# Interleaving LayerNorm and its transposes with the Q, K and V projections, tile by tile, in an eight-core transformer layer on Trainium2

## The reference

```python
xn = _layernorm(x, axis=-1)
s = attn(xn, qw, kw, vw, ow)   # 16 heads of 64, rope on Q and K, causal softmax
g = _silu(moe(xn, Wg, We, be)) # 8 experts of 1024 x 1024, top 2 by xn @ Wg.T
x = x + s * g
```

## Time and profile before

| what | value |
|---|---|
| time, median of 3 runs | 3062.99 us (3062.61 to 3220.71) |
| the profiled execution | 3064.13 us |
| its span, first to last instruction, slowest core | 3062.6 us |
| spans of the eight cores | 3039.6 to 3062.6 us |
| PE / DVE / ACT / POOL busy | 72% / 35% / 32% / 18% |
| mean granted clock of PE | 0.873 of full speed |

### The profile page before, as it was taken

The page is one execution under the profiler, slowest core; times in us unless marked ns, Lnnn a source line. Parts: engine busy times, 40 slices in busy tenths (PEclk is TensorE's granted clock), DMA queues, the critical chain, the costliest instruction groups (busy, mean ns, idle before and its releaser), DMA issues.

```text
span 3062.6 us, 30462 instructions; the slowest of 8 cores (3039.6 to 3062.6 us)
## 1 busy us (share of the span) xinstructions
PE 2195.3 (72%) x9976; PEld 819.0 (27%) x9976; DVE 1066.2 (35%) x1560; ACT 965.4 (32%) x1373; POOL 539.9 (18%) x575
## 2 busy tenths in 40 slices
PE   1233498888499689959969990677778807777787
PEld 0113133333144234424424440112121201121212
DVE  3661466666244234414423440322121203121212
ACT  3550122222100200020020000565758504757584
POOL 0010178888100000000000000211111102211111
PEclk9999999999699799979979995588888856788888
DMA  4159522222733255073335408022010080220100
GB/s 128 45 76 111 70 97 104 104 104 104 138 56 56 64 91 94 1 137 56 56 77 94 78 1 209 12 69 69 1 56 1 1 194 1 69 69 1 55 1 28
DMA packets 380489, 212.37 MB, mean 69 GB/s; under 512 B 342944, under 2 KB 342944, under 8 KB 379824
## 3 DMA queue, kind: packets, MB, share of 16 engines
q1 hardware_dynamic: 365552, 142.76, 22.6%
q0 software_dynamic: 14784, 67.66, 10.1%
HBM read 92.67 MB, written 67.37 MB: 52 GB/s over the span
## 4 chain that ended last, share of the span: by engine, by line
PE 44%; DVE 12%; ACT 11%; SPq 8%; issue 8%; POOLq 5%; DMA 5%; POOL 5%; DVEq 0%; ACTq 0%
PE PA L654 15%; PE PB L654 14%; ACT AR L838 8%; SPq L238 7%; PE PV L757 5%; POOLq L92 5%; POOL AR L849 5%; PE PA L883 4%; DMA AR<-c_sin 3%; PE PA L828 2%; PE PB L828 2%; DVE AR L550 2%; ACT AR L767 2%; DVE AR L556 2%; DVE AR L548 2%
## 5 line engine op out<-in xcount | busy, mean ns | idle before, releaser
L654 PE MATMUL PA<-AR 128*128 128x512 f16 x2048 | 469.9, 383 | 23.8 <-DMA AR<-we 23.8
L757 PE MATMUL PV<-AR 128*128 128x512 f16 (+6 forms) x1280 | 416.6, 416 | 66.4 <-POOL AR L849 66.3
L654 PE MATMUL PB<-AR 128*128 128x512 f16 x2048 | 462.9, 379 | 0.0
L838 ACT ACTIVATE AR<-PA 128x1024 f16<-128x1024 f32 x320 | 303.2, 948 | 250.6 <-PE PA L828 248.5
L828 PE MATMUL PA<-AR 64*128 64x512 f16 x640 | 148.7, 456 | 300.4 <-DMA AR<-q_sp 145.8
L664 DVE SCALAR_TENSOR_TENSOR AR<-PA,wm,AR 128x512 f32<-128x512 f32 x256 | 192.1, 750 | 423.1 <-PE PA L654 222.3
L849 POOL TENSOR_TENSOR AR<-AR,tri 128x256 f16<-128x256 f16 x256 | 171.2, 669 | 821.3 <-ACT AR L838 797.8
L838 ACT ACTIVATE AR<-PB 128x1024 f16<-128x1024 f32 (+1 forms) x320 | 276.3, 864 | 90.4 <-PE PB L828 90.3
L664 DVE SCALAR_TENSOR_TENSOR AR<-PB,wm,AR 128x512 f32<-128x512 f32 x256 | 192.1, 750 | 249.3 <-PE PB L654 230.9
L654 PEld LDWEIGHTS PA<-AR 128*128 128x128 f16 x2048 | 202.0, 99 | 271.5 <-issue 34.9
L799 DVE TENSOR_TENSOR AR<-AR,PC 64x512 f16<-64x512 f32 x64 | 43.5, 680 | 661.8 <-PE PC L793 660.6
(11 more groups left out here) (99 smaller groups left out, 1923.5 us busy)
## 6 DMA issues: line engine op xcount, KB each, us to landing
we<-we POOLq DMA_DIRECT2D x8, 2048.0 KB, 87.7
out_c<-AR SPq DMA_DIRECT2D x8, 2048.0 KB, 10.3
v_sp<-AR POOLq DMA_DIRECT2D x32, 264.0 KB, 3.2
AR<-v_sp POOLq DMA_DIRECT2D x2, 4224.0 KB, 28.5
AR<-x_c POOLq DMA_DIRECT2D x32, 256.0 KB, 3.1
AR<-c_cos SPq DMA_DIRECT2D x32, 256.0 KB, 2.7
AR<-c_sin SPq DMA_DIRECT2D x32, 256.0 KB, 3.0
q_sp<-AR SPq DMA_DIRECT2D x32, 256.0 KB, 2.1
```

The lines of the kernel that those rows point to most:

```text
L654: sl=slots[ib], half=half: e.matmul(PG[:, 512 * ib:512 * ib + 512], lhs, sl[:, c * D + half * 512: c * D + (half + 1) * 512], start=(c == ...
L757: nkc=nkc, p2=p2, mw=mw: e.matmul(PV2[0:mw, 512 * p2 + w0:512 * p2 + 512], v_sb[:, kc * VF + h * VW:kc * VF + h * VW + mw], expb3[sbk][:, ...
L838: W("scalar", lambda e, PS=PS, sbk=sbk, ev=ev: e.activation(ev(expb3[sbk]), ev(PS), AF.Exp, scale=1.0 / 32.0), waits=[("eT", C["eT"]), ("e ...
```

## The change

LayerNorm and QKV become one loop over turns `it`. In a turn come: step 1 of LayerNorm for tile it, step 6 (the transposes) for tile it-5, steps 2 to 5 for tiles it-1 to it-4, on every second turn from 12 on one of the eight expert weight casts, and the whole QKV work of tile it-6, now a function `p1_tile`. Router logits and routing follow behind the last tile, and the two barriers stand one after the other behind them. So that both can be in work together, the LayerNorm buffers get their own place in AR2 (1 KB larger), the transposes go to the two banks of PV2, and the centred x is written as f16 once, in `xcn16`, which is scaled in place: the f32 buffer and the f32-to-f16 copy go. A QKV matmul waits for the transposed copies of its own tile. The copy of the logits out of PC6 stands there twice.

```diff
-        xst = [c16(AR2, 71680 + 2048 * i, 1024) for i in range(4)]
-        xc32 = [c32(AR2, 79872 + 4096 * i, 1024) for i in range(4)]
-        sqd = c32(AR2, 96256, 1024)
-        xn16 = [c16(AR2, 100352 + 2048 * i, 1024) for i in range(4)]
+        xst = [c16(AR2, 90624 + 2048 * i, 1024) for i in range(4)]
+        xcn16 = [c16(AR2, 98816 + 2048 * i, 1024) for i in range(4)]
+        sqd16 = c16(AR2, 107008, 1024)
...
             W("scalar", lambda e, q=q: e.activation(
-                xc32[q][:, :], xst[q][:, :], AF.Identity,
+                xcn16[q][:, :], xst[q][:, :], AF.Identity,
                 bias=mneg[q][:, :], scale=1.0),
               waits=[("eV", tok[("mnegd", q)]),
-                     ("eV", tok.get(("xc16", q), 0))], inc="eA")
+                     ("eT", tok.get(("xnrd", q), 0))], inc="eA")
...
-            W("vector", lambda e, q=q: e.tensor_copy(xn16[q][:, :],
-                                                     xc32[q][:, :]),
-              waits=[("eV", C["eV"]), ("eT", tok.get(("xnrd", q), 0))],
-              inc="eV")
-            tok[("mrd", q)] = C["eV"]
             W("vector", lambda e, q=q: e.tensor_scalar(
-                xn16[q][:, :], xn16[q][:, :], rc32[q][:, :], None,
+                xcn16[q][:, :], xcn16[q][:, :], rc32[q][:, :], None,
                 op0=ALU.mult),
-              waits=[("eV", C["eV"])], inc="eV")
+              waits=[("eV", C["eV"]), ("eA", tok[("sqdone", q)])], inc="eV")
             tok[("xc16", q)] = C["eV"]
 
-        tp16 = [PC6.bitcast(F16)[:, 0:128], PC7.bitcast(F16)[:, 0:128]]
+        PV2f16 = PV2.bitcast(F16)
+        tp16 = [PV2f16[:, 0:128], PV2f16[:, 1024:1152]]
...
-        dma("gpsimd", we16[0, :, :], we_h[0, :, :], "swe")
-        for ei in range(1, NE):
-            dma("gpsimd", we16[ei, :, :], we_h[ei, :, :], "swe")
-        dma("gpsimd", be16s[0:8, :], be_h[:, :], "sbe")
...
+                    for bi3 in range(3):
+                        wts = [("sw3", w3), ("eV", tok[("xnTv", gt)]),
+                               ("eA", tok[("xnTa", gt)])]
+                        if c == 0:
+                            wts.append(("eA", tok.get(("pjev", grp), 0)))
+                            if grp == 1 and bi3 == 2:
+                                wts.append(("eA", wgT_done))
...
+        for it in range(NT + 6):
+            if it < NT:
+                ln_s1(it)
+            if 5 <= it < NT + 5:
+                ln_s6(it - 5)
+            if 1 <= it < NT + 1:
+                ln_s2(it - 1)
+            if 2 <= it < NT + 2:
+                ln_s3(it - 2)
+            if 3 <= it < NT + 3:
+                ln_s4(it - 3)
+            if 4 <= it < NT + 4:
+                ln_s5(it - 4)
+            if 12 <= it < 12 + 2 * NE and (it - 12) % 2 == 0:
+                ei = (it - 12) // 2
+                dma("gpsimd", we16[ei, :, :], we_h[ei, :, :], "swe")
+            if it == 12 + 2 * NE:
+                dma("gpsimd", be16s[0:8, :], be_h[:, :], "sbe")
+            if it >= 6:
+                p1_tile(it - 6)
...
+        W("vector", lambda e: e.tensor_copy(lgall[:, :], PC6[:, 0:256]),
+          waits=[("eT", C["eT"]), ("eV", C["eV"])], inc="eV")
```

More of the change, by code:

```diff
@@ L136, in build_nc @@
         AR1 = sbt("AR1", [128, 65536], U8)
-        AR2 = sbt("AR2", [128, 110592], U8)
+        AR2 = sbt("AR2", [128, 111616], U8)
         def c16(ar, off, cols):
@@ L148, in build_nc @@
         attnT = c16(AR1, 49152, 8192)
-        xst = [c16(AR2, 71680 + 2048 * i, 1024) for i in range(4)]
-        xc32 = [c32(AR2, 79872 + 4096 * i, 1024) for i in range(4)]
-        sqd = c32(AR2, 96256, 1024)
-        xn16 = [c16(AR2, 100352 + 2048 * i, 1024) for i in range(4)]
-        lgall = c32(AR2, 108544, 256)
-        l2a = c32(AR2, 109568, 256)
+        xst = [c16(AR2, 90624 + 2048 * i, 1024) for i in range(4)]
+        xcn16 = [c16(AR2, 98816 + 2048 * i, 1024) for i in range(4)]
+        sqd16 = c16(AR2, 107008, 1024)
+        lgall = c32(AR2, 109056, 256)
+        l2a = c32(AR2, 110080, 256)
         qwS = c16(AR2, 0, 8192)
@@ L283, in build_nc @@
         wgT_done = C["eA"]
+        wgT_tp = C["eT"]
+        w3 = C["sw3"]
         SSP = ("sspA", "sspB", "sspC", "sspD")
@@ L306, in ln_s2 @@
             W("scalar", lambda e, q=q: e.activation(
-                xc32[q][:, :], xst[q][:, :], AF.Identity,
+                xcn16[q][:, :], xst[q][:, :], AF.Identity,
                 bias=mneg[q][:, :], scale=1.0),
               waits=[("eV", tok[("mnegd", q)]),
-                     ("eV", tok.get(("xc16", q), 0))], inc="eA")
+                     ("eT", tok.get(("xnrd", q), 0))], inc="eA")
             tok[("xcd", q)] = C["eA"]
             W("scalar", lambda e, q=q: e.activation(
-                sqd[:, :], xc32[q][:, :], AF.Square, accum_out=ssum[q][:, :]),
+                sqd16[:, :], xcn16[q][:, :], AF.Square,
+                accum_out=ssum[q][:, :]),
               waits=[("eA", C["eA"]), ("eV", tok.get(("vrd", q), 0))],
@@ L358, in ln_s6 @@
                 W("tensor", lambda e, q=q, c=c, bp=bp: e.transpose(
-                    tp16[bp][:, :], xn16[q][:, c * 128:(c + 1) * 128],
+                    tp16[bp][:, :], xcn16[q][:, c * 128:(c + 1) * 128],
                     idn[:, :]),
@@ L407, in build_nc @@
                           stop=(c == NCH - 1 and s3 == 2)),
-                      waits=[("eV", xnT_evV), ("eA", max(wgT_done, xnT_evA))],
-                      inc="eT")
+                      waits=[("eA", max(C["eA"] if t == 0 and c == 0 and s3 == 0 else 0, wgT_done))], inc="eT")
+        W("vector", lambda e: e.tensor_copy(lgall[:, :], PC6[:, 0:256]),
+          waits=[("eT", C["eT"]), ("eV", C["eV"])], inc="eV")
         d3 = lambda a: a.rearrange("q (t e) -> q t e", e=8)
```

244 lines of the change are left out of this document (121 added, 123 removed).

## The result

The changed kernel is slower: its runs take about 3432 us (3430.1 to 3432.9), and those of the kernel before that were taken beside them about 3069 (3061.2 to 3085.8). The ratio is 1.118, with a 95% interval of 1.115 to 1.121. The forecast was 3428, from a start of 3063. The profiled execution took 3432.74 us. Its span is 3431.2, so 369 longer than before.

What follows compares the result with a forecast made beforehand. The prediction took a closed chain of waits through PE, ACT, POOL's x load and DVE to bound the merged loop. Its terms put the expert start at 1152.8 us, against 787.9: 3063 + 365 = 3428 us, range 3335 to 3515.

Steps and rivals of the forecast that it cites:

- The closed chain: Merged loop: matmuls, rope, x load, row sum, DVE copies and transposes wait in a circle; 33.4 us a turn.
- The signs that the prediction named: Changed profile: PE about 40% busy, about 6 us idle DVE behind each rope, PE wait of some 18 us before third transpose.
- 25 turns with an x load: Merged loop, before tiles 1 to 25: each turn includes waiting for an x load; 25 x 33.42 = 835.5 us.
- cost of the casts, apart: Eight expert-weight casts inside the loop, costing PE waits for instructions; 20 us taken, between bounds of 0 and 78.
- 5 turns without one: Before tiles 26 to 30: no x load left, DVE goes from rope straight to copies; 5 x 25.75 = 128.8 us.
- logits: Router logits behind the loop: their busy time of 22.5 us, without the earlier waits for instructions.
- expert start: Time when the expert stage begins: forecast 1152.8 us, against 787.9 before the change.
- The landing of x: Step of each chain turn: x load from issue to landing on POOL's queue, 3.1 us.
- The slow start of each tile: PE restarts at low clock after each wait: 12.5 us of matmuls a tile; always warm would save 31 x 2.08 = 64 us.
- Rival 1: Casts collide with the loads in the loop, each delaying the chain by its whole 19.3 us: 154 us, 3562; 8 in 100.
- Rival 2: The x load is hidden and copies follow DVE's rope directly: 192 us less, 3236 us; 4 in 100.
- Rival 3: Interleaving works, some 15 us a tile: expert start 625 us, a gain of 163, 2900 us; 3 in 100.

Runs made afterwards that it cites:

- experiment 2: Changed kernel with the rope and stores of a tile written one turn later, behind the next tile's matmuls; ratio 0.978 to the kernel before, expert start 703.8 us.
- experiment 10: Changed kernel with x loaded a turn earlier and transposes spread between matmuls and copied by ACT, rope in its old place; ratio 0.958, expert start 652.9 us.
- experiment 1: Changed kernel with each x load issued one turn earlier on POOL's queue; ratio 1.066 to the kernel before, expert start 974.6 us.
- experiment 5: Changed kernel with the eight expert-weight casts moved to turns 30 to 37, one in each; ratio 1.122 to the kernel before, expert start 1161.2 us.
- Experiment 4: Changed kernel with 84 unread matmuls (42 in the last turns) filling PE's wait behind the second transpose; 3406.9 us in one comparable run.
- experiment 7: Kernel before, nothing merged, with only the casts moved: one at every second QKV tile from tile 6 on; ratio 1.011, expert start 845.3 us.
- experiment 8: Late rope and early x load as in experiment 3, each cast cut into four of 0.5 MB, one a turn from turn 6; ratio 0.937.
- experiment 9: As experiment 3, with the next tile's transposes in pairs between matmuls, copied by ACT, and LayerNorm steps 2 to 5 between matmul groups; ratio 0.935.
- experiment 11: The spread transposes of experiment 9 together with the quartered casts of experiment 8; ratio 0.910 to the kernel before, 2790 to 2797 us.
- experiment 3: Changed kernel with both the x load one turn earlier and the rope one turn later; ratio 0.957 to the kernel before, 2925 to 2948 us.

## Why the prediction was right, point by point

The closed chain, the claim on which all else rests, is shown from two sides. Its waits are in the trace of the changed kernel, and experiments 2 and 10 open it, each at another place. They take 458 us away (from the changed kernel) and 322 (from experiment 1), without removing work. The signs that the prediction named came too: PE busy for 43% of the loop, 7.7 us of idle DVE behind each rope, ended by the load of x, waits of up to 22 us before the third transpose. The sum, against landmarks of the changed kernel's trace:

| term | forecast | measured | difference |
|---|---|---|---|
| first QKV matmul | 71.3 | 67.2 | -4.1 |
| 25 turns with an x load | 25 x 33.42 = 835.5 | 25 x 34.78 = 869.5 | +34.0 |
| cost of the casts, apart | 20 | in the turns | -20 |
| 5 turns without one | 128.8 | 125.6 | -3.2 |
| last two tiles, last copies | 25.2 | 24.4 | -0.8 |
| logits | 22.5 | 25.5 | +3.0 |
| routing and barriers | 49.5 | 49.9 | +0.4 |
| expert start | 1152.8 | 1162.0 | +9.3 |
| the rest | 2274.7 | 2269.2 | -5.5 |

That the whole came out within 4 us is in part luck. The forecast turns were 34 us too short in all, and the 20 for the casts and 5.5 in the rest happened to stand against it. The slowest core also matters: the other seven reached the expert start 6 to 19 us before it.

- **The landing of x was the term most off in size.** I took 3.1 us from the earlier trace rows; in the loop it was 3.2 to 6.7, with a median of 4.5. DVE's wait for it is 193.1 / 25 = 7.7 us where my terms give 11.47 + 3.1 - 8.65 = 5.9, so 1.8 more a turn. The other terms are a little under: in the turn shown, row sum to first copy 1.69 (1.85 forecast) and first copy to the next matmul 2.11 (2.30). The matmuls took 12.39 (12.5).
- **The casts cost less than the 20, and in another way.** I had bounded them by waits for instructions, and none came. Turns with a cast took 36.0 us, those without 34.2, so 8 x 1.8 = 14 us on this core; on others the difference was as low as 0.3 a turn, and experiment 5 gives 13 on the slowest cores and 2.6 on the mean. The way is the x load: issued directly ahead of a cast, it landed after 5.5 to 6.7 us, in the other turns after 3.2 to 5.4. That both share the DMA engines is my reading of it. The 20 was near in size by luck, as its reason was not the one that acts. The rest of the +34, some 20 us, is x landing later than 3.1 in turns without a cast, too.
- **The slow start of each tile** held, for 30 tiles (the second to the 31st). The trace shows a granted clock of 0.50 at the end of every wait and over the first 2.5 us of matmuls (0.50 to 0.53), and about 0.43 us per matmul. Experiment 4 gives the price: its warm tiles took 10.4 us, 2.0 less than the mean, against 2.08 in the forecast. The Trainium skill, "TensorE: Matmul & The Clock Gate", section "HAM oscillation — how this bites in real kernels", says that each burst after such an idle wait pays anew; the series of 30 tiles agrees.
- **The logits** were 3.0 us over. Without the waits of the earlier trace rows they take 25.5 us, where I took the busy time of 22.5. The low clock (0.54 in place of 1.00) is not the reason: in experiment 7 they ran at 1.00 and took 25.5 us as well. The busy time of a stretch with long waits was not the time that the work takes without them; why the matmuls follow each other more closely behind a wait is open.
- **Rival 1** (casts collide, 154 us) falls for this kernel: 14 us at most. Its reason was sound elsewhere, as experiment 7 measures 101 us in a stage with turns of 12.7 us. This fits my ground against it, that the turn of 33 us gives a cast time to end, but no run varies the length of the turn alone.
- **Rival 2** (x is hidden) falls: DVE idles between rope and row sum in all 25 turns. Experiment 1 shows what it would have been worth, 187 us for my 192.
- **Rival 3** (the overlap works) falls for the order as written. By another order experiments 8, 9 and 11 reach its expert start of 625 and pass it (580, 597 and 514); experiments 2, 3 and 10 come near.

The rest of the kernel, from the expert stage on, was forecast unchanged; it is 5.5 us shorter. No run explains this, and the range of 22 us over kernels that share it says that a difference of this size tells nothing.

## What to carry to other kernels

When two stages are merged into one loop, write down for each engine the order of one turn and follow the waits once around: if the first thing that PE needs next stands behind the last thing that another engine does with PE's newest result, the loop is serial, whatever the busy shares say. Put short copies that free a buffer ahead of long work on the newest tile, and issue loads a turn before they are read. And when the loop has become short, spread large background transfers over many turns in pieces (experiment 8).

## What the runs showed of the hardware that was not expected

- Beside DRAM-to-DRAM casts of 2 MB on POOL's queue, a load of sines on SP's queue took up to 16.7 us to land where 3.0 is usual, and the QKV stage lost 12.6 us for each cast (experiment 7). As four pieces of 0.5 MB, one a turn, no turn over 16.2 us remained (experiment 8).
- One program, one execution, two paces: turns of up to 16.98 us on six cores at a granted clock of 0.74 to 0.76, and of 13.68 on two at 1.00 (experiment 3, 100 to 140 us). Denser kernels, with the casts in quarters, held 1.00 on all eight. The cause stays open.
- PE's waits for instructions in the logits came where casts ran beside them: 34.8 us before, 14.4 in experiment 5, none in the changed kernel.
- The 768 matmuls of 128x8 took 25.5 us at a granted clock of 0.54 (changed kernel) and at 1.00 (experiment 7), while those of 128x512 took half the time at the higher clock: one started every 0.43 us at 0.50, and every 0.22 us in a warm tile (48 in 10.4 us).
